# The last unit of the second dense layer ahead of the logits in TensorE's stream

## The reference

```python
xn = _layernorm(x)
x = x + attn0(xn) + ffn0(xn)      # linear attention + sliding window; dense layers, below
xn = _layernorm(x)
x = x + attn1(xn) + experts(xn)   # causal attention; 8 experts, the best 2 of each token

# ffn0
h = silu(tlin(x, w1_w, w1_s)) * tlin(x, w2_w, w2_s)     # 128 -> 512
h = gelu(tlin(h, h1_w, h1_s))                            # 512 -> 512, "h1" in the kernel
h = gelu(tlin(h, h2_w, h2_s))                            # 512 -> 512, "h2": the second dense layer
return tlin(h, w3_w, w3_s)                               # 512 -> 128, "third_layer"

# experts
logits = xt @ Wg.T
topk_logits, topk_idx = top_k(logits, 2)
w = softmax(topk_logits)                                 # the gates
y = einsum('te,teh->th', gates, gelu(xt @ W1 + b1) @ W2 + b2)
```

## Time and profile before

| | |
|---|---|
| median of 3 runs | 1298.84 us (1294.39 to 1299.34) |
| the profiled execution, own time | 1290.89 us |
| its span, first to last instruction | 1289.1 us |
| mean granted TensorE clock | 0.965 |
| PE busy | 1165.4 us (90%) |
| DVE busy | 865.2 us (67%) |
| ACT busy | 743.5 us (58%) |
| POOL busy | 649.6 us (50%) |
| chain that ended last | PE 49%, DVE 21%, ACT 13%, issue 8%, POOL 6% |

### The profile page before, as it was taken

The page is one execution under the profiler, slowest core; times in us unless marked ns, Lnnn a source line. Parts: engine busy times, 40 slices in busy tenths (PEclk is TensorE's granted clock), DMA queues, the critical chain, the costliest instruction groups (busy, mean ns, idle before and its releaser), DMA issues.

```text
span 1289.1 us, 26679 instructions
## 1 busy us (share of the span) xinstructions
PE 1165.4 (90%) x9122; PEld 750.8 (58%) x9122; DVE 865.2 (67%) x3433; ACT 743.5 (58%) x1580; POOL 649.6 (50%) x846
## 2 busy tenths in 40 slices
PE   5989999999999899989998999899989867988997
PEld 2445754565457545754575457545764456884896
DVE  4066588658865885688658865786578755885563
ACT  2356367735773577457745774477546624557675
POOL 4475254535444454545454544454445436675577
PEclk9998999999999899999999999899989969999999
DMA  7601620162015301540154015401472016542233
GB/s 237 153 3 54 177 73 12 54 184 73 13 55 147 108 15 39 151 120 15 39 152 117 17 39 151 117 17 39 139 211 64 5 26 142 82 70 29 41 55 40
DMA packets 123961, 105.53 MB, mean 82 GB/s; under 512 B 15242, under 2 KB 118578, under 8 KB 123826
## 3 DMA queue, kind: packets, MB, share of 16 engines
q1 hardware_dynamic: 102162, 85.89, 24.7%
q0 software_dynamic: 13792, 9.54, 5.1%
q10 hardware_dynamic: 7872, 8.39, 1.9%
HBM read 58.59 MB, written 46.37 MB: 81 GB/s over the span
## 4 chain that ended last, share of the span: by engine, by line
PE 49%; DVE 21%; ACT 13%; issue 8%; POOL 6%; DMA 2%; DVEq 0%; SPq 0%; POOLq 0%; ACTq 0%
PE bank L700 14%; PE heads L765 11%; ACT probs L1117 8%; PE bank L679 6%; PE bank L707 6%; DVE xnT_s L1585 4%; DVE hrow L1585 4%; DVE hT_s L1585 3%; POOL out L1362 3%; PE bank L690 2%; PE bank L675 2%; DVE spare L1585 2%; PE bank L1050 2%; PE bank L684 1%; PE bank L815 1%
## 5 line engine op out<-in xcount | busy, mean ns | idle before, releaser
L1117 ACT ACTIVATE probs<-bank 128x512 f32<-128x512 f32 (+2 forms) x896 | 441.2, 582 | 176.6 <-PE bank L707 169.8
L1309 POOL TENSOR_SCALAR_AFFINE_SELECT probs<-probs 128x384 f32<-128x384 f32 x256 | 127.7, 521 | 242.1 <-ACT probs L1117 242.1
L765 PE MATMUL heads<-probs,V 128*18 128x192 f32 (+9 forms) x3072 | 194.6, 394 | 10.7 <-POOL probs L1312 4.6
L707 PE MATMUL bank<-K,Q 128*128 128x192 bf16 (+4 forms) x1024 | 199.2, 271 | 4.3 <-ACT probs L1117 0.2
L707 PE MATMUL bank<-Q,K 128*128 128x192 bf16 (+4 forms) x1024 | 175.0, 275 | 16.3 <-ACT probs L1117 7.0
L1362 POOL DMA_INDIRECT out<-h1T_s x78 | 123.2, 1580 | 60.3 <-ACT h1T_s L1270 37.4
L765 PEld LDWEIGHTS heads<-probs,V 128*9 128x9 f32 (+1 forms) x3072 | 78.2, 94 | 122.3 <-issue 85.4
L1262 ACT ACTIVATE h2T_s<-bank,h1T_s 128x128 f32<-128x128 f32 x312 | 89.2, 368 | 93.1 <-PE bank L1050 80.9
L707 PEld LDWEIGHTS bank<-Q,K 128*128 128x128 bf16 x1024 | 81.4, 99 | 87.5 <-ACT probs L1117 31.1
L707 PE MATMUL bank<-QM,K 128*128 128x512 bf16 (+3 forms) x512 | 121.5, 301 | 7.8 <-DVE gatesT_s L1545 1.4
L707 PEld LDWEIGHTS bank<-K,Q 128*128 128x128 bf16 x1024 | 85.2, 98 | 67.7 <-DVE mx_c L1585 14.3
(11 more groups left out here) (241 smaller groups left out, 2285.1 us busy)
## 6 DMA issues: line engine op xcount, KB each, us to landing
K<-slots_of_k SPq DMA_DIRECT2D x64, 256.0 KB, 4.2
Q<-slots_of_q SPq DMA_DIRECT2D x15, 1024.0 KB, 10.9
QM<-slots_of_qm SPq DMA_DIRECT2D x8, 1024.0 KB, 9.4
h1T_s<-sorted_rows SPq DMA_DIRECT2D x78, 65.0 KB
slots_of_q<-Q SPq DMA_DIRECT2D x8, 384.0 KB, 2.6
slots_of_k<-QM SPq DMA_DIRECT2D x8, 384.0 KB, 2.9
slots_of_qm<-Q SPq DMA_DIRECT2D x8, 384.0 KB, 2.6
slots_of_k<-Q SPq DMA_DIRECT2D x8, 384.0 KB
```

Source lines behind the costliest of these rows:

```text
L707: mm = pe.matmul(to[:, at:at + right.shape[1]], left, right, start=True, stop=True, skip_group_check=True)
L765: mm = pe.matmul(heads[ROWS * i:ROWS * i + n, P * j:P * j + widths[j]], V[:, j, g // 2, i, first:first + n], slot_of(kind, 2 * g + i // 2) ...
L1117: return act.activation(to, bank, func, scale=scale, bias=bias).then_inc(taken_sem(run, unit), 1)
L1309: pool.affine_select(out=three, in_=three, compare_op=ALU.is_ge, fill=0.0, base=0, pattern=[[0, 3], [1, P]], channel_multiplier=-1)
```

## The change

TensorE's program computes `h2_3` right behind `v2`, ahead of the wait for `xnT2` and of the logits, where it did so behind the logits. The list of units is changed in the same way. Both changes act in the first round and the six steady ones. In the last round there is no `h2_3`, and `run_tiles` keeps its place. The opening has its own code (`first_dense`), which stays.

```diff
@@ dense_order
-    units += ["hT2", "k2", "q2", "xnT2", "v2", "logits"] if this else []
+    units += ["hT2", "k2", "q2", "xnT2", "v2"] if this else []
     units += ["h2_3"] if after else []
+    units += ["logits"] if this else []
     return units
@@ dense_stage of TensorE
                 pe.wait_ge(S["xn2"], due("xn2", now, 1))
                 turn(run, "xnT2", lambda t: xn[:, t, :])
                 project_rows(run, "v2", hT, wv1[:, :])
+                if after:
+                    dense_low(run, "h2_3", layer2, 3)
                 wait_taken(run, "xnT2")
                 project_rows(run, "logits", xnT, wgT[:, :], E)
-                if after:
-                    dense_low(run, "h2_3", layer2, 3)
-                else:
+                if not after:
                     run_tiles(QUERIED, ROUTED)
```

## The result

| | before | changed |
|---|---|---|
| median, 4 runs each | 1299.04 us (1294.39 to 1299.34) | 1279.83 us (1278.45 to 1281.25) |
| ratio, 95% interval | | 0.9865 (0.9844 to 0.9885) |
| profiled execution, own time | 1290.89 us | 1279.02 us |
| its span | 1289.1 us | 1277.3 us |
| its mean granted clock | 0.965 | 0.974 |

The changed kernel is 19.2 us faster by the medians, 11.9 us by the two profiled executions. The forecast, 1282.1 us for the profiled execution and 1290.0 for the median, was 3.1 us off the one and 10.2 off the other. Between the two comparisons the changed kernel's median moved by 1.4 us, that of before by 4.1.

The account below looks back on a forecast made before the run. Bound: TensorE's stall for the xnT_s copy, then half-rate h2_3, in seven places, with TensorE and VectorE waiting in turn. 15.1 - 6.3 = 8.8 us off: 1282.1 us profiled, 1290.0 median; range 1282.5 to 1298.

Parts of the forecast that it names:

- The step that failed: From profiled execution to median: the median's 0.6% excess was assumed to stay, turning 1282.1 us into 1290.0.
- the short stretch: Half rate behind the logits' stall for 3.3 us, in three of seven rounds; the change gains 3.7 us there together.
- 15.1 less 6.3 us: Seven dense-stage ends: 15.1 us from earlier first maxima, 6.3 given back through the clock, leaving 8.8 us off.
- not 7.0: VectorE's first row maximum was to start 7.0 us behind the end of v2 in all seven places.
- The give-back: Half rate behind TensorE's new gap slows scores and third layer: 0.9 us per round, 6.3 us in all.
- My own reading of the rows: TensorE's new gap of some 2.3 us lowers the clock, being nearer to 2.41 us (fell) than 1.93 (held).
- the slower case: Rival: the long low stretch hits first maxima and third layer every round; 8 us slower, 1306.8 us; chance 0.08.
- The clock didn't hold: Judges the rival that the clock holds behind the new gap: whole 15.1 us stay, 1283.7 us; chance 0.20.
- The queries' transfer: Rival: the first causal scores wait for its landing; about 2 us of gain stay, 1297 us; chance 0.17.
- POOL's rows: VectorE waits 0.6 us for them at its slot reduction, inside its old 1.06 us third-layer wait: cost nothing.

Follow-up runs that it names:

- e1: The kernel before, run once more with no edit, 12 executions: 1296.49 us, ratio 0.9988 to its neighbours.
- e4: The changed kernel plus ten unused matmuls in TensorE's new gap behind the seventh unit of scores: 1276.61 us, ratio 0.9844 to before.
- e9: The changed kernel, run once more with no edit, six executions: 1281.19 us, ratio 0.9903 to before.
- e7: The kernel before in its old order plus 4 unused matmuls in the stall ahead of the logits: 1281.81 us, ratio 0.9897 to before.
- e3: The changed kernel with 8 of h2_3's 12 matmuls ahead of the logits and 4 behind: 1278.32 us, ratio 0.986 to before.
- e11: The kernel before in its old order, with only the third layer moved ahead of the fifth maximum: 1288.60 us, ratio 0.9963 to before.
- e10: The changed kernel with TensorE's wait for the copy of xnT_s moved ahead of h2_3: 1305.08 us, ratio 1.009 to before.
- e2: The kernel before in its old order plus ten unused matmuls in the stall ahead of the logits: 1275.57 us, ratio 0.9837 to before.
- e5: The changed kernel with the third layer moved from ahead of the ninth maximum to ahead of the fifth: 1268.26 us, ratio 0.9800 to before.
- e6: The changed kernel with 4 of h2_3's 12 matmuls ahead of the logits and 8 behind: 1275.66 us, ratio 0.985 to before.

## Why the prediction was right or wrong

**The step that failed** is "the median of the runs shown is 1298.84, 0.6% above the profiled one; I take the same difference from it". The difference between the two is no constant. It is the same clock that the sum is about: the profiled execution had three rounds with the short stretch, e1's, near the median, two, and the second stretch in four rounds instead of two. The changed kernel had the short one in 13 of the 14 places of its two profiles. So a median of before loses more by the change than the profiled one, 17.1 us from e1's span to the changed one's, where it was 11.8 from the first profile's. The changed kernel's own median lies only 0.8 us above its profiled execution, where this step put 7.9. Of the 10.2 us by which the forecast missed the median, this step makes 7.1; the other 3.1 were already missing in the forecast for the profiled execution, and they are the second stretch and the begin (below), less the 1.7 us in the tail. The range ended at 1282.5 and the time lies under it.

**The mechanism at the place held, its sum partly by luck.** 15.1 less 6.3 us made 8.8; copy to gates lost 8.7 us between the profiles that the sum was made for. But both terms were too small by about as much. The first maximum comes 549.99 - 543.33 = 6.7 us behind v2 and not 7.0, since h2_3 begins ahead of v2's end: over the seven places it comes 17.2 us earlier, not 15.1. The give-back is 1.0 to 1.4 us per round at the third layer, not 0.9; e4, which fills the gap, puts it at 8.7 us for all seven and not 6.3. That the difference came out right is luck.

**The second term left out** is the stretch near the start of h1, 1.4 us each time, of which the first profile had two. I saw a clock of 0.965 and looked for its stretches only at the place of the change. Whether the change removes them is not shown: of the changed kernel's two profiles one has none and e9's has one, but e4, with no stall and no gap, has four. They are 3.3 of the 11.8 us, and their cause stays open, as does the begin of the span (1.5 us), ahead of the first place that the change touches.

**The clock.** That the gap lowers it was right in seven rounds of seven, and e4 shows it by filling the gap. The Trainium skill's advice in "TensorE: Matmul & The Clock Gate", section "Why this matters for your kernels", which would have passed a gap of this size, is not borne out by any of the seven. My own reading of the rows, that 2.3 us is nearer to 2.41 (falls) than to 1.93 (holds), gave the right answer by a wrong rule: in e7 1.48 us lowered the clock and 1.83 did not, in e3 a gap of 1.5 did, and two stalls of 2.41 us in e11, three of 2.41 and one of 2.76 in e10 did not. The length of one stall does not decide, and seven of seven was not the rule that it looked like. What does decide is not shown.

**The rivals.** The low stretch stayed at 3.4 us in 13 of 14 places, so the slower case fell. The clock didn't hold. The queries' transfer was harmless at this point: no wait for it stands in the changed kernel's rows. In the round at 546 it was issued at 549.8 and landed 8.4 us later, at 558.2, and the first causal scores started at 559.44. But part of that lead comes from the slow third layer, which holds the scores back. Where the third layer runs at full rate or earlier, some rounds wait for the landing: 0.4 us in one round of e4, 0.1 to 1.8 in three of e2, 0.7 to 1.4 in four of e5. The rival was real, and comes up as the rounds get shorter. POOL's rows cost VectorE 0.7 us, of which only 0.16 is a wait. The rest is one multiplication that ran beside POOL's copy of the rows. First POOL's timeline of the changed kernel, then VectorE's:

```profile
553.15 1.03 POOL L1340 COPY rows<-xn 128x1024 f32<-128x1024 f32 x1
```

```profile
553.48 0.79 DVE L1676 TENSOR_TENSOR place<-place,picks 128x64 f32<-128x64 f32 x1
```

It took 0.22 us in the kernel before, where it came behind the copy, and 0.79 here: it ends 0.1 us behind POOL's copy, at 554.3. The Trainium skill, "SBUF — State Buffer", section "SBUF: two separate sides", says that VectorE and GpSimd share one pair of ports, which one instruction holds to its end; the trace agrees, with these 0.57 us. All of it lay in the wait for the third layer, as foreseen.

**Where the gain at the place is from** is shown from four sides: filling the stall without changing order gives all of it (e2), the old order with its stall unfilled is as fast to the first maximum wherever the clock happens to hold (e11), changing the order without covering the stall turns it round (e10), and with partial covers it goes by whether the clock held (e6, e7). The idle time itself was not on the path, as the logits wait for the copy in any order. What cost was half rate: h2_3 at 4.2 to 5.3 us instead of 2.9, and the logits ahead of it at up to 1.9 instead of 1.1.

## What to carry to other kernels

A stall of a few microseconds on TensorE is not priced by its length but by whether the clock falls behind it, which can differ from one execution to the next, and by what stands there: work that a neighbour's wait hides at full rate comes out of hiding at half rate. Put real matmuls into it, and look where the next gap opens; the third layer in that gap (e5) was worth some 12 us more, and opened the next wait. Before a sum is set against a median, look at the mean granted clock of several executions: if they differ, one profile doesn't stand for them.

## What the runs showed of the hardware

- Executions of one unchanged kernel on one core spread by 1%, in step with their mean granted clock: 1286.57 us at 0.968 to 1299.71 at 0.956 (e1), while the changed kernel's six of e9 lie within 0.12%, and all ten of its executions within 0.26%.
- A stall of 1.83 us left the clock at 1.00 and one of 1.48 us in the same execution was followed by 0.50 (e7). Of seven stalls of 2.41 and 2.76 us with the same work around them two left it at 1.00 (e11).
- The 12 matmuls of 512 columns took 2.85 us at 1.00 and 5.10 at 0.50. The third layer's 32, of 128 columns, took 3.74 us at full rate and 3.9 to 5.2 where half rate lay over part of them.
